# Slot rows read ahead of the shared rows' store, four weight places filled behind them, blank sums one tile ahead

## The reference

```python
x = _layernorm(x + attn(x))
router_logits = x @ gate_w
topk_w, topk_ids = _grouped_topk(router_logits, bias)       # 6 of 64 experts
y = _routed_moe(x, topk_w, topk_ids, w_gate, w_up, w_down)  # silu(b@wg) * (b@wu) @ wd, by slots
shared = silu(x @ ws_gate) * (x @ ws_up) @ ws_down
out = _layernorm(x + y + shared)
```

## Time and profile before

| | us |
|---|---|
| median of 3 runs | 1075.36 (1070.57 to 1077.23) |
| the profiled execution's own time | 1073.27 |
| its span | 1071.5 |
| PE busy | 965.9 (90%) |
| DVE busy | 681.1 (64%) |
| ACT busy | 488.6 (46%) |
| POOL busy | 371.8 (35%) |

### The profile page before, as it was taken

One profiled execution on the slowest core, in us unless ns is written; L12 is line 12 of the kernel. 1 busy time (PEld: TensorE's weight loads), 2 busy tenths in 40 slices (PEclk: granted clock), 3 DMA queues, 4 the chain that ended last, 5 costly groups with the idle time before them and its releaser, 6 DMA issues.

```text
span 1071.5 us, 16751 instructions
## 1 busy us (share of the span) xinstructions
PE 965.9 (90%) x5240; PEld 739.3 (69%) x5240; DVE 681.1 (64%) x1703; ACT 488.6 (46%) x1083; POOL 371.8 (35%) x334
## 2 busy tenths in 40 slices
PE   8999979989999999999979999999999998559745
PEld 6888867667787778776767667888787776336412
DVE  5989853775766675757565668575857666424326
ACT  4012124555656564645544456564645544125402
POOL 4878863234323121021244332312031112126811
PEclk9999988999999999999979999999999999769968
DMA  8696765463222111111243224351112133978687
GB/s 254 228 289 218 250 230 159 127 165 110 73 64 61 60 52 58 45 33 50 85 133 90 84 74 132 87 156 45 56 31 69 44 79 99 274 214 194 86 279 284
DMA packets 137303, 137.24 MB, mean 128 GB/s; under 512 B 18065, under 2 KB 108805, under 8 KB 137216
## 3 DMA queue, kind: packets, MB, share of 16 engines
q1 hardware_dynamic: 84064, 98.33, 30.1%
q10 hardware_dynamic: 43872, 29.50, 9.4%
q0 software_dynamic: 9280, 8.34, 4.5%
HBM read 86.44 MB, written 63.05 MB: 140 GB/s over the span
## 4 chain that ended last, share of the span: by engine, by line
PE 67%; DVE 10%; issue 8%; SPq 5%; DMA 5%; ACT 2%; POOL 2%; ACTq 1%; DVEq 0%; POOLq 0%
PE s_ps L1116 14%; PE ring L1126 9%; PE o_ps L1146 8%; PE o_ps L1143 8%; PE ring L1155 7%; PE s_ps L1095 6%; PE ring L1095 5%; DVE neg_max L1319 2%; SPq L759 2%; PE s_ps L1209 2%; PE o_ps L1095 2%; SPq L655 1%; PE s_ps L1119 1%; DVE pt_lo L1253 1%; DMA inverses<-inv_t 1%
## 5 line engine op out<-in xcount | busy, mean ns | idle before, releaser
L1319 DVE TENSOR_REDUCE neg_max<-s_ps 128x1 f32<-128x128 f32 (+7 forms) x256 | 191.6, 750 | 137.6 <-PE s_ps L1119 131.8
L961 ACT ACTIVATE probs<-s_ps,neg_max 128x128 f32<-128x128 f32 (+7 forms) x256 | 189.7, 741 | 142.3 <-DVE neg_max L1319 127.8
L1116 PE MATMUL s_ps<-kt,qt_hi 128*128 128x512 f32 (+3 forms) x768 | 235.2, 388 | 6.0 <-ACT probs L961 3.9
L824 POOL TENSOR_TENSOR qt_lo<-q_raw,qt_hi 128x512 fp32r<-128x512 f32 x64 | 82.1, 1283 | 319.3 <-ACT qt_hi L875 319.0
L1126 PE MATMUL ring<-ident,probs 128*128 128x128 f32 x1152 | 177.5, 277 | 9.2 <-DVE pt_lo L1253 5.1
L875 ACT ACTIVATE pt_hi<-ring 128x512 fp32r<-128x512 f32 x168 | 99.8, 596 | 181.8 <-PE ring L1126 173.6
L1116 PEld LDWEIGHTS s_ps<-kt,qt_hi 128*128 128x128 f32 x768 | 139.7, 194 | 54.9 <-issue 30.2
L1253 DVE TENSOR_TENSOR pt_lo<-ring,pt_hi 128x512 fp32r<-128x512 f32 x168 | 115.4, 687 | 62.2 <-ACT pt_hi L875 56.7
L1126 PEld LDWEIGHTS ring<-ident,probs 128*128 128x128 f32 x1152 | 129.1, 142 | 33.7 <-issue 14.5
L1146 PE MATMUL o_ps<-pt_hi,v 128*128 128x512 f32 x336 | 145.9, 435 | 1.4 <-DVE pt_lo L1253 0.9
L1116 PE MATMUL s_ps<-kt,qt_lo 128*128 128x512 f32 (+3 forms) x384 | 134.6, 350 | 0.0
(11 more groups left out here) (201 smaller groups left out, 1378.8 us busy)
## 6 DMA issues: line engine op xcount, KB each, us to landing
qk_rows<-prods SPq DMA_DIRECT2D x80, 256.0 KB, 2.8
q_raw<-qk_rows ACTq DMA_DIRECT2D x128, 128.0 KB
inv_row<-inverses SPq DMA_DIRECT2D x64, 256.0 KB
fsum<-sums SPq DMA_DIRECT2D x48, 256.0 KB, 8.1
sums<-blank SPq DMA_DIRECT2D x16, 640.0 KB
wexp<-in_L_ffn_w_gate_dram SPq DMA_DIRECT2D x32, 192.0 KB, 5.0
wexp<-in_L_ffn_w_up_dram SPq DMA_DIRECT2D x32, 192.0 KB, 5.2
wexp<-in_L_ffn_w_down_dram SPq DMA_DIRECT2D x32, 192.0 KB, 6.3
```

The lines of the kernel that those rows point to most:

```text
L961: act.activation(probs[:, u % 2, h, 0:blocks(u) * P], s_ps[:, n % 2, score_cols(n)], ACT.Exp, bias=neg_max[:, n % 8:n % 8 + 1], accum_out= ...
L1116: pe.matmul(s_ps[:, n % 2, c + a:c + e], q[qp], k[kp][:, a:e], start=(qp == kp == 0), stop=(qp == 1 and not last))
L1319: dve.tensor_reduce(neg_max[:, n % 8:n % 8 + 1], s_ps[:, n % 2, score_cols(n)], AX_X, ALU.max, negate=True).then_inc(max_ready, 1)
```

## The change

Three edits. On SyncE the blank sums are written one tile ahead: two tiles' at tile 0, one at each of tiles 1 to 14, none at tile 15. The load of weights at the last `outproj` stops after 7 pairs, and the other 4 are issued after the store of `z_sb`, when the second chunk of slot rows has landed. On ScalarE the wait for `z_stored` moves from ahead of the first three loads of slot rows to behind them.

```diff
+BEFORE_ROUTING = 7
 ...
                     sp.wait_ge(var_ready, s[1] + 1)
                     if s[1] + XB < TILES:
                         load_x(TILES + s[1] + XB)
-                    blank_sums(s[1])
+                    for i in range(s[1] + 1 if s[1] else 0, min(s[1] + 2, TILES)):
+                        blank_sums(i)
 ...
                 if s == ("outproj", TILES - 1):
 
                     sp.wait_ge(pv_done, PT_ALL)
-                    load_homes(kt[0], v_sb[0], kt[1], v, q_raw, qt_hi, qt_lo, probs, pt_hi, pt_lo)
+                    load_homes(kt[0], v_sb[0], kt[1], v, q_raw, qt_hi, qt_lo, probs, pt_hi, pt_lo, most=BEFORE_ROUTING)
                 if s[0] == "zadd":
                     i = s[1]
                     read(sp, ("sd", i))
                     sp.dma_start(sums[i * P:(i + 1) * P, :], z_sb[:, :]).then_inc(z_stored, 16)
             sp.wait_ge(attn_ready, TILES)
+            sp.wait_ge(srow_loaded[1], 16)
             load_homes(kt[0], v_sb[0], kt[1], v, q_raw, qt_hi, qt_lo, probs, pt_hi, pt_lo, ot)
             sp.wait_ge(z_stored, 16 * TILES)
 ...
             act.activation(act_cell[:, :], minus_half[:, :], ACT.Sigmoid)
-            act.wait_ge(z_stored, 16 * TILES)
             for n in range(2):
                 act.wait_ge(scattered[n], 8 * K * TILES)
 ...
             for g in range(3):
                 load_slots(g)
+            act.wait_ge(z_stored, 16 * TILES)
```

## The result

The changed kernel takes 1071.55 us (median of 20 runs, 1065.84 to 1075.54), the kernel before 1075.18 (20 runs). The medians differ by 3.6 us. The ratio, which is estimated from all runs and not from the two medians, is 0.9963 with a 95% interval of 0.9946 to 0.9981, or 2.0 to 5.8 us less: clear of no change, and under one per cent. The profiled execution took 1066.11 us, with a span of 1064.3.

A forecast was written before the change was run, and what follows sets the result against it. It took SyncE's queue ahead of the slot loads, then GpSimd's accumulates, as the bound. A start 3.9 us earlier less 2.2 given back made -1.7: 1073.7 against the median, put at 1073 us, range 1068 to 1078.

The forecast's parts named there:

- What bounds: After attention, SyncE's queue of weights and the z_sb store delay the slot loads; GpSimd's accumulates end the expert stage.
- The wait moved: On ScalarE, the first slot load then waits for the scatters alone; worth 1.2 to 1.7 us with the weights as before.
- The start: Weights cut to 7 pairs: slot loads go out and PE starts 3.9 us earlier, bounds 1.7 and 6.5.
- The give-back: Four late pairs delay GpSimd's accumulates in the expert stage: accumulate 3 waits, 2.2 us lost, bounds 0 and 6.7.
- Those behind it issue at the pace of the landings or 1.76: Accumulates after number 3 follow at landing pace or 1.76 us each, the queue having emptied.
- What it loses here it doesn't get back: GpSimd is the slowest of the expert stage, so the 2.2 us lost at the accumulates stays lost.
- The blank sums: Nothing more gained at tile 15; the write added at tile 0 costs 0, at most 2.4 us.
- Full conversion: Rival: the four pairs don't hold the accumulates; net -3.9, to -6.5, 1069 to 1071.5 us; chance 0.25.
- The wait of 0.3: Accumulate 3's wait if engines take turns between queues and only the weights' queue is beside it; landing 5.6 us.
- Contention wins: Rival: several rounds of accumulates lose 2.3 us each, loss above 3.9 us; at 6.7 net +2.8, 1078.2; chance 0.15.
- Scatters late of themselves: Rival: last scatters land late at their own pace; start 1.7 us earlier at best, net 0, 1075; chance 0.13.
- Tile 0: Rival: the second blank write holds inv_row or q's load, PE loses up to 2.4 us, net +0.7; chance 0.05.

The follow-up runs named there:

- four kernels that release all four pairs at once: The changed kernel, twice; it with blank sums at their own tile; it with ScalarE's wait where it was. Ratios to before 0.9963, 0.9969, 0.9964, 0.9952.
- nine ahead: The changed kernel with 9 pairs of weights ahead of the z_sb store and 2 behind, not 7 and 4; ratio to before 0.9923, run again 0.9974.
- four kernels with 11 ahead: The kernel before; it with only the blank sums early; with only the wait moved; with both. Ratios to before 1, 1.0002, 0.9988, 0.9975.
- four left out: The changed kernel without the loads of pairs 24 to 27, which use the weights of pairs 20 to 23; ratio to before 0.9945.
- nine ahead again: The second run of the changed kernel with 9 pairs ahead of the z_sb store and 2 behind; ratio to before 0.9974.
- eleven ahead: The changed kernel with all 11 pairs ahead of the z_sb store, wait moved and blank sums ahead kept; ratio to before 0.9975.
- one by one: The changed kernel with the four late pairs released one at a time, at pairs 1, 3, 5 and 7 of ScalarE's scaled rows; ratio to before 0.9964.
- the wait kept: The changed kernel with ScalarE's wait for z_stored left ahead of the slot loads; ratio to before 0.9952.

## Why the prediction was right, step by step

1073 us with 1068 to 1078 was forecast, 1071.55 measured. The net of the forecast was -1.7 us, its own case -0.5 to -3; the medians differ by 3.6. The mechanism is the one of the forecast: an earlier start, and part of it given back in the accumulates. Both terms were sized too small, by 1.4 us at the start and by about 1.1 in the price (3.3 for 2.2); they have opposite signs, and that the time came out so near is partly luck.

*What bounds.* Right: cutting the weights that were moved ahead of the store and beside the scatters moved the start, and GpSimd's last accumulate still ends the stage (chain above).

*The wait moved: 1.2 to 1.7 us.* Too much. Alone it gave A 0.6 us, lost again in a slower slot load; with 7 pairs it gave nothing.

*The start: 3.9 us.* It was 5.3 (11.12 - 5.78); the first slot load would be at 941.9 on the old trace's time, and 943 to 944 was named as the sign. The mis-sized part is the landing of the last scatter: 3.56 us, taken from an accumulate's row, against 2.07 measured. The bound below was the scatter's own end at 0.97, so 2.07 lay inside. An accumulate adds up to 96 rows of 1 KB to what stands in DRAM; the last scatter wrote next to no bytes (48 packets, 0.00 MB). It was a poor neighbour for the estimate. For the store of z_sb the same 3.6 was taken, and 1.8 measured; that held nothing.

*The give-back: 2.2 us.* Placed rightly, at accumulate 3, and too small there: the idle time ahead of it is 3.86, 3.80, 4.21 and 4.98 in the four kernels that release all four pairs at once, each with the 0.30 that is always there. The 7.6 us of landing that was used comes from one pair beside a slot chunk; four pairs beside two chunks made it 8.9, counted in the same way.

"Those behind it issue at the pace of the landings or 1.76" missed the second round. Accumulate 6 is held as well in all four, and starts 15.8 to 16.8 us behind number 0, before 10.9. By then 4.9 to 5.9 us are lost. "What it loses here it doesn't get back" was wrong too: by accumulate 9 the loss is 2.3 to 3.2 us (21.1 to 22.1 us behind number 0, before 18.8), since the wait of accumulate 8 in the kernel before doesn't come again. At accumulate 31 it is 1.6 to 4.1. So the price isn't one wait that stays; waits come earlier, and a part of them was paid before too.

*The blank sums: 0.* Right for the changed kernel, with nothing to spare. At tile 0 the two writes are one after the other, and the next inv_row load went out 5.2 us behind the store of its row, not 2.7 (the earlier trace rows have that load), as the 2.4 us of the working say:

```profile
191.25 1.00 SPq L673 DMA_DIRECT2D sums<-blank  x2
...
199.61 0.35 SPq L724 DMA_DIRECT2D inv_row<-inverses  x1
...
203.30 0.69 DVE L1343 TENSOR_TENSOR ot<-o_ps,inv_row 128x512 f32<-128x512 f32 x1
```

Its reader starts 3.7 us behind it without a wait, and 3.7 us is what the load takes to land, not the 3.0 of a slot load that was used. In the second kernel with nine ahead, which has the same blank sums, the reader did wait:

```profile
204.33 0.69 DVE L1343 TENSOR_TENSOR ot<-o_ps,inv_row 128x512 f32<-128x512 f32 x1 [0.73 <-DMA inv_row<-inverses]
```

*The rivals.* Full conversion gave a time near the measured one (1071.5) for the wrong reason: the four pairs cost 3.3 us, and only a start better than forecast covers it. The wait of 0.3 that stood beside it was worked out for the weights' queue alone; here the slot chunks were loading too and the idle time was 3.86, and no run has one queue of weights alone against the accumulates, so it stays untested. Contention wins: its mark, a loss above 3.9 us, was nearly reached in one kernel and passed in two (S0 3.7, 4.0 and 4.1 above before), and the second held round that it names is there, at accumulate 6; but the gain at the start was 5.3 and not 3.9. Scatters late of themselves: refuted by 2.07 us on free engines beside 6.82 and 6.16 on full ones. Tile 0: not seen in the changed kernel, 0.73 us of VectorE's time in one profile of nine ahead.

Over the profiles, the start from the z_sb add to accumulate 0 gains 5.7 us (mean of the four kernels with 11 ahead 23.1, of the four with 7 released at once 17.4) and S0 loses 3.3, so 2.4 are left; the run times say 3.3 to 5.2. The rest, some 1 to 3 us, is within what single profiles differ by, and stays open.

## What to carry to other kernels

A wait that the chain names may have a second one right behind it: ask what else has to pass the same full DMA engines before counting on its removal. Here the bytes ahead mattered and not the wait. Transfers that are put off to free a queue come back in the next stage, and there they cost whoever has a fixed number of transfers in flight; price them by the landing times of that stage under load. Estimate a landing from a transfer of the same kind and bytes, not only of the same queue.

## What was not expected of the hardware

An indirect transfer that moved next to nothing took 2.07 us to land on free DMA engines and 6.2 to 6.8 while another queue kept them full. The Trainium skill, page "DMA: Bandwidth & Descriptors", section "Queues, rings and completion order", says that the increment that reports a transfer lands only after every earlier write of that engine, across its queues. The trace agrees with that and with the mere taking of turns; no run here tells the two apart.

TensorE's clock doesn't come back at the same time in each execution, and a short wait of PE goes with a late return. PE had been nearly idle, at 0.50 (1.2 GHz), and both kernels below work the same pairs; from 5 us behind PE's first transpose the changed kernel has it at 0.95 (near 2.4 GHz), and the one with four left out at 0.50 and only then at 0.95 (columns: stretch, us, PE busy, PEclk, DMA share, GB/s). First the changed kernel:

```profile
946.59:949.09 2.50, 2.50 (x22) 0.95 1.10 309
```

and four left out, two stretches:

```profile
947.36:949.86 2.50, 2.50 (x15) 0.50 0.01 3
949.86:952.36 2.50, 2.48 (x21) 0.95 0.22 31
```

What differs ahead of it is chunk 1 of the slot rows, which pair 2 needs. In the changed kernel it has landed when PE comes to it; in four left out PE waits:

```profile
945.61 0.70 PE L1203 MATMUL s_ps<-ident,srow 128*128 128x128 f32 x2 [0.39 <-DMA srow<-slot_rows]
```

Four of the fourteen profiles have this wait on PE's own row: four left out 0.39 us, nine ahead again 0.42, eleven ahead 0.66, one by one 0.98. They are the four whose clock is still 0.50 from 5 to 7.5 us behind the first transpose, and the four with the latest accumulate 0, 9.7 to 10.3 us behind it. In nine others it stands at 7.7 to 8.7 us, and the clock of that stretch is 0.75 or more; the wait kept lies between (9.05 us, 0.63). So a landing of chunk 1 that is late by under 1 us moves accumulate 0 by some 2 us, as much as the effects that were looked for. That the wait is the cause of the late clock is an inference from these profiles; no run took it alone, and none tried a smaller chunk 1. A length that begins at PE's start holds this; one that begins at accumulate 0 doesn't.
